# Two attentions moved from three-part bf16 rows to F32R row strips, with three single banks for first-pass scores and a ring of four for second scores

## The reference

```
Q = (query @ Wq.T).reshape(B, QL, HEADS, HEAD_DIM)
scores = einsum('bqhd,khd->bhqk', Q, K) * SCALE
attn = softmax(scores, axis=-1)
out = einsum('bhqk,khd->bqhd', attn, V)
```

## Time and profile before

| | |
|---|---|
| median of 3 runs | 2120.23 us (2119.72 to 2126.68) |
| profiled execution | 2117.09 us, its span 2115.3 us |
| granted TensorE clock, mean | 0.925 |
| busy: PE, DVE, ACT, POOL | 85%, 66%, 54%, 14% |
| a0: first matmul, first second-pass matmul, last work | 88.57, 112.17, about 885 us |
| a1: block starts, first second-pass matmul, last work | 1035.3, 1054.2, about 1287 us |

### The profile page before, as it was taken

How to read it: one execution, slowest core, us unless ns; L and a number is a source line. 1 busy time by engine, 2 the same in 40 slices (tenths; PEclk the granted TensorE clock), 3 DMA queues, 4 the chain that set the end, 5 groups by cost and what they waited for, 6 DMA issues and landing times. The chain is left out here.

```text
span 2115.3 us, 31356 instructions
## 1 busy us (share of the span) xinstructions
PE 1808.1 (85%) x9772; PEld 970.4 (46%) x9772; DVE 1399.7 (66%) x1846; ACT 1147.7 (54%) x2253; POOL 285.7 (14%) x447
## 2 busy tenths in 40 slices
PE   4499999999999999645699973499999999949997
PEld 3122222222222233133222221388888888748886
DVE  6487777877777888246467753666666666656665
ACT  3067767776777777513377762255445454424432
POOL 3210000000000000102111111211111111002223
PEclk8599999999999999856799986799999999979999
DMA  7201111111111200112312222100000000023432
GB/s 284 96 34 35 40 46 35 41 39 36 35 39 35 89 16 16 36 56 55 112 65 70 72 101 73 39 14 20 7 20 20 20 12 10 1 51 115 121 105 65
DMA packets 56274, 115.00 MB, mean 54 GB/s; under 512 B 7249, under 2 KB 21585, under 8 KB 54123
## 3 DMA queue, kind: packets, MB, share of 16 engines
q1 hardware_dynamic: 53715, 109.21, 15.9%
q10 hardware_dynamic: 2456, 4.46, 0.8%
HBM read 83.52 MB, written 30.12 MB: 54 GB/s over the span
## 5 line engine op out<-in xcount | busy, mean ns | idle before, releaser
L348 DVE TENSOR_REDUCE a_max_part<-psum 128x1 f32<-128x1024 f32 x640 | 759.6, 1220 | 253.8 <-PE psum L265 253.8
L389 ACT ACTIVATE a_probs<-psum 128x512 f32<-128x512 f32 x1280 | 675.1, 603 | 247.9 <-PE psum L309 242.7
L265 PE MATMUL psum<-a_k_rows,a_q_rows 96*128 96x512 bf16 x1280 | 399.6, 395 | 52.0 <-DMA a_q_rows<-q_parts 26.1
L309 PE MATMUL psum<-a_q_rows,a_k_rows 99*128 99x512 bf16 x1280 | 410.3, 386 | 29.6 <-ACT a_probs L389 29.3
L300 PE MATMUL psum<-a_probs,a_v_ext 128*32 128x512 f32 x2560 | 342.5, 607 | 6.1 <-ACT a_o_out L373 3.8
L265 PEld LDWEIGHTS psum<-a_k_rows,a_q_rows 96*128 96x128 bf16 x1280 | 98.8, 98 | 407.0 <-issue 193.0
L309 PEld LDWEIGHTS psum<-a_q_rows,a_k_rows 99*128 99x128 bf16 x1280 | 124.1, 98 | 268.8 <-ACT a_probs L389 155.4
L1548 PE MATMUL psum<-high_t_parts,high_gu 128*128 128x512 f32 x600 | 145.6, 393 | 6.8 <-DVE high_t_parts L1642 6.8
L1253 PE MATMUL psum<-wide_k_t,wide_q_t 128*128 128x512 f32 (+3 forms) x576 | 130.3, 353 | 1.7 <-DVE wide_id_bf L1452 1.7
L1548 PEld LDWEIGHTS psum<-high_t_parts,high_gu 128*128 128x128 f32 x600 | 113.6, 190 | 31.3 <-issue 7.3
L226 POOL TENSOR_TENSOR a_max_bf<-a_neg_max,a_zeros 128x4 bf16<-128x4 f32 x64 | 13.2, 206 | 849.0 <-DVE a_neg_max L352 849.0
(11 more groups left out here) (173 smaller groups left out, 1871.1 us busy)
## 6 DMA issues: line engine op xcount, KB each, us to landing
o<-a_o_out SPq DMA_DIRECT2D x64, 256.0 KB, 2.1
gu_in<-in_w_gu SPq DMA_DIRECT2D x25, 256.0 KB, 3.0
k_parts<-keys_parts SPq DMA_DIRECT2D x12, 512.0 KB, 6.5
a_k_rows<-k_parts SPq DMA_DIRECT2D x16, 384.0 KB
high_cw<-cw SPq DMA_DIRECT2D x24, 256.0 KB, 3.9
setup_k_in<-in_k SPq DMA_DIRECT2D x4, 1024.0 KB, 15.2
a_k_rows<-k_parts SPq DMA_DIRECT2D x16, 256.0 KB
a_v_in<-in_v SPq DMA_DIRECT2D x16, 256.0 KB, 14.8
```

The source lines that it names most:

```text
L265: mm = pe.matmul(psum[:, 2 * (n % 2) + j, :], q_rows[0:KROWS, b, q0:q0 + P], k_rows[0:KROWS, b, k0:k0 + 512], start=True, stop=True)
L309: pe.matmul(psum[:, bank_of(filling(j)), :], k_rows[0:SROWS, b, j * P:(j + 1) * P], q_rows[0:SROWS, b, half * QH:(half + 1) * QH], start=T ...
L348: dve.tensor_reduce(max_part[:, u % 2, c // nch, c % nch:c % nch + 1], psum[:, 2 * (n % 2):2 * (n % 2) + 2, :], AX.XY, ALU.max).then_inc(s ...
L389: act.activation(probs[:, j % pring, :], psum[:, bank_of(filling(j)), :], ACT.Exp).then_inc(exp_done, 1)
```

## The change

Keys and queries are no longer cut into bf16 parts. Each is cut in two F32R parts, high and low. A strip of 64 partitions holds three products of 16 rows each (48 rows, 51 with the maxima): high times high, high times low and low times high. The first half of a head's keys lies in the strip at partition 0, the second half in the strip at partition 64, and consecutive matmuls alternate between strips.

- GpSimd makes the key parts of each head (`split_keys`: three operations over `nkt * 64` columns), head by head, from a single buffer `k_in` that SP fills with four transfers (`load_k`); `setup` has no key split any more. `copy_v` works from a single buffer `v_in` too.
- The first pass uses three single banks (0 to 2) and reductions over 512 columns. The second pass has a ring of four banks (3 to 6).
- ScalarE copies the maxima into `max_row`, and SP moves them beside the queries by two transfers (`send_maxima`).
- VectorE, not ScalarE, copies out the sums (`take_sums`).
- TensorE's order inside a group is `slot`. All loops are written out. Resident heads: 3 in a0, 6 in a1. SP loads the sums of 15 heads before the last two units.
- In a0 the queries stay in SBUF and are spread by six transfers a head; in a1 they pass through DRAM, two transfers a head.

```diff
+        self.per_strip = nkt * P // 2
+        self.steps = nkt
+        self.shift = 12
+        self.turn_at = nkt - 6
+        self.ring = 4
+        self.first_ring = 3
+        self.early = 2
...
+    def load_k(self, sp, h):
+        keys = self.k_dram[HD * h:HD * h + HD, :]
+        for n in range(2):
+            part = keys[:, n * self.per_strip:(n + 1) * self.per_strip]
+            at = STRIP * n
+            sp.dma_start(self.k_in[at:at + 2 * HD, :],
+                         part.unsqueeze(0).broadcast_to([2, HD, self.per_strip])).then_inc(self.k_loaded, 16)
+            sp.dma_start(self.k_in[at + LOW_K:at + MROW, :], part).then_inc(self.k_loaded, 16)
...
+    def split_keys(self, pool, h):
+        b = h % self.nb
+        pool.wait_ge(self.k_loaded, 64 * (h + 1))
+        pool.tensor_tensor(self.k_rows[:, b, :], self.k_in[:, :], self.zeros[:, 0:1].broadcast_to([P, self.per_strip]),
+                           ALU.add).then_inc(self.k_high, 1)
+        pool.wait_ge(self.k_high, h + 1)
+        for s in range(2):
+            low = slice(STRIP * s + LOW_K, STRIP * s + MROW)
+            pool.tensor_tensor(self.k_rows[low, b, :], self.k_in[low, :], self.k_rows[low, b, :],
+                               ALU.subtract).then_inc(self.k_split, 1)
...
+        def heads_split(u):
+            return min(H, self.early + u + 1, nb + u // 2)
...
+            sent = self.early + 1
+            send_maxima(0)
+            for u in range(us):
+                h, half = u // 2, u % 2
+                if u + 1 < us:
+                    send_maxima(u + 1)
+                sp.wait_ge(self.o_full, u + 1)
+                sp.dma_start(self.o_dram[h, :, half * QH:(half + 1) * QH], self.o_out[:, half, :]).then_inc(self.o_stored[half], 16)
+                if half == 1 and h + nb < H:
+                    load_q(sp, q_rows[:, h % nb, :], h + nb, self.q_loaded[h % nb])
+                while sent < min(H, heads_split(u) + 1):
+                    sp.wait_ge(self.k_split, 2 * sent)
+                    self.load_k(sp, sent)
+                    sp.wait_ge(self.v_ready, sent)
+                    self.load_v(sp, sent)
+                    sent += 1
+                if u == us - 3:
+                    for n in range(2):
+                        sp.wait_ge(self.o_stored[n], 16 * (H - 1))
+                    load_sums(sp, o4, self.o_dram, 0, H - 1, self.o4_loaded)
...
+            for u in range(us):
+                if u + 1 < us:
+                    split_max(u + 1)
+                for h in range(done, heads_split(u)):
+                    self.copy_v(pool, h)
+                    self.split_keys(pool, h)
+                done = heads_split(u)
...
+            def first_chunk(n):
+                u, c = n // steps, n % steps
+                if n >= self.first_ring:
+                    pe.wait_ge(self.s1_free, n - self.first_ring + 1)
...
+                second_wait(u, j)
+                second_wait(u, j + 1)
+                second_chunk(u, j)
+                second_chunk(u, j + 1)
+                if one < self.chunks:
+                    first_chunk(one)
+                    first_chunk(one + 1)
+                if j + 2 == self.turn_at and u + 1 < us:
+                    turn_maxima(u + 1)
+                second_wait(u, j + 2)
+                second_chunk(u, j + 2)
+                if one < self.chunks:
+                    first_chunk(one + 2)
+                second_wait(u, j + 3)
+                second_chunk(u, j + 3)
+                if one < self.chunks:
+                    first_chunk(one + 3)
+                if g > 0:
+                    pv_group(u, g - 1)
+                elif u > 0:
+                    pv_group(u - 1, groups - 1)
...
+            for u in range(us):
+                for s in range(steps):
+                    if s == 4 and u > 0:
+                        take_sums(u - 1)
+                    n = u * steps + s + ahead
+                    if n < self.chunks:
+                        first_pass_chunk(n)
```

More of the change, by code:

```diff
@@ new lines, in _ @@
+            pool.wait_ge(self.v_const, 2)
+            self.copy_v(pool, 0)
+            for h in range(1, self.early):
+                self.split_keys(pool, h)
+                self.copy_v(pool, h)
+            done = self.early
+            split_max(0)
+            for u in range(us):
+                if u + 1 < us:
+                    split_max(u + 1)
+                for h in range(done, heads_split(u)):
+                    self.copy_v(pool, h)
+                    self.split_keys(pool, h)
+                done = heads_split(u)
@@ L330, in _ @@
[L330 to L341 removed]
+                mm.then_inc(self.pv_done, 1)
@@ new lines, in slot @@
+            def slot(u, g):
+                j = group * g
+                one = u * steps + 4 * g + ahead
+                second_wait(u, j)
[19 more added lines that the diff above has]
+                    pv_group(u - 1, groups - 1)
@@ new lines, in _ @@
+            put_row(0)
+            for u in range(us):
+                for j in range(nkt):
+                    p = u * nkt + j
+                    if j == self.turn_at and u + 1 < us:
+                        put_row(u + 1)
+                    act.wait_ge(self.s2_full, p + 1)
+                    if p >= self.pring and p % group == 0:
+                        act.wait_ge(self.pv_done, (p - self.pring) // group + 1)
+                    act.activation(self.probs[:, p % self.pring, :], psum[:, self.bank_of(u, self.filling(j)), :],
+                                   ACT.Exp).then_inc(self.exp_done, 1)
@@ new lines, in project, with _ @@
+        if q_out is not None:
+            @block.sync
+            def _(sp):
+                heads = P // HD
+                for c in range(DC):
+                    sp.wait_ge(high_done, 2 * c + 2)
+                    sp.wait_ge(low_done, 2 * c + 2)
+                    for at, src in ((0, q_high), (HD, q_low), (2 * HD, q_high)):
+                        sp.dma_start(q_out[heads * c:heads * (c + 1), at:at + HD, :], src[:, c, :].bitcast(F32)).then_inc(stored, 16)
+                for c in range(DC):
+                    sp.wait_ge(k_taken, 2 * c + 2)
+                    sp.dma_start(k_out[c * P:(c + 1) * P, :], k_sb[:, c, :]).then_inc(stored, 16)
@@ L1700, in adaln_two_layers, with load_q @@
-            project(nc, psum, "p0", h_t, wq, 1, [q0_parts], None, keys_stored, 16 * 3 * 4)
-        with ExitStack() as part:
-            o4 = part.enter_context(nc.sbuf_tensor("o4_0", [P, DC, 4, T], F32))
-            attention_core(nc, psum, ident_bf, "a0", nk0 // P, 4, k0_parts, q0_parts, i["v0"], o0, o4)
-            merge_heads(nc, psum, "m0", 4, o4, o0, den0, i["wo0"], gates[:, 0, :], x)
+            o4 = part.enter_context(nc.sbuf_tensor("o4_0", [P, DC, 4, T], F32))
+            with ExitStack() as core:
+                attention = Attention(nc, core, psum, ident_bf, "a0", nk0 // P, 3, i["k0"], i["v0"], o0)
+                q_high = core.enter_context(nc.sbuf_tensor("q_high", [P, DC, T], F32R))
+                q_low = core.enter_context(nc.sbuf_tensor("q_low", [P, DC, T], F32R))
+                def load_q(sp, rows, h, loaded):
+                    at = HD * (h % 8)
+                    for n in range(2):
+                        for m, src in enumerate((q_high, q_low, q_high)):
+                            row = STRIP * n + HD * m
+                            sp.dma_start(rows[row:row + HD, :].bitcast(F32), src[at:at + HD, h // 8, :].bitcast(F32)).then_inc(loaded, 16)
+                with ExitStack() as front:
+                    setup(nc, psum, i["c"], i["wmod"], i["ident"], ident, ident_bf, mod_col, mod_row, gates, i["x"], x,
+                          i["ln_w"], ln_w[:, :], attention)
+                    wq = front.enter_context(nc.sbuf_tensor("wq", [P, DC, 1, D], F32))
+                    normalise(nc, psum, "n0", x, ident, False, mod_col[:, 2:4], mod_col[:, 0:2], h_t,
+                              loads=[(wq[:, :, 0, :], chunks(i["wq0"]))])
+                    project(nc, psum, "p0", h_t, wq, 1, q_high, q_low)
+                with nc.Block() as block:
+                    attention.run(block, load_q, 6, o4)
```

591 lines of the change are left out of this document (229 added, 362 removed).

## The result

The changed kernel takes 2273.62 us (median of 4 runs, 2270.23 to 2276.41). Beside it on the same chip the kernel before took 2120.32 (2119.72 to 2126.68). The ratio is 1.0715, 95% interval 1.0689 to 1.0741. It is 153 us slower; the forecast was 108 us slower, 2228, with a range up to 2285.

What follows compares the result with a forecast made beforehand. TensorE, busy 99% in a0's steady part, was read as the bound before the change. The terms 11 - 10 - 14.5 + 15 + 113 - 6 = +108.5 gave 2228 us against the median, range 2130 to 2285.

Steps and rivals of the forecast that it cites:

- Part 1: a0's groups: one chain of first-pass matmuls, reduction and values, 3.0 us a group against 2.90; +11 us (-18 to +40).
- the wait behind the sums: Before a0's last unit: its maxima stand behind the sums of 15 heads in SP's queue; +15 us (0 to +18).
- The jumps' 10 us: a0's loop: the two jumps back, 5.2 us each, go; -10 us.
- Part 2: Start of a0: block 10 us earlier, second pass begins 39 us after it, at 97.5; -14.5 us (-20 to -8).
- load until about 15, 13.6: Start of a0: head 1 loaded until about 15 us after the block, then GpSimd's key split takes 13.6 us.
- maxima through SP, 4.5: Start of a0: moving the first maxima through SP takes 4.5 us before the second pass begins.
- Part 4: a1: maxima wait behind sums and loads in SP's queue, early units also for GpSimd; 364 against 251 us, +113 (+60 to +145).
- A: a1 and before the last units: maxima never late, a1's units 6.3 us, 2081 us in all; chance 0.13.
- B: a0: VectorE sets the pace, 21.6 us a unit, -73 in place of +11, 2144 us in all; chance 0.13.
- F3's wait: a0's group: the fourth first-pass matmul waits until VectorE has reduced the group's first, since there are three banks.
- C: a0: changing between strips costs TensorE 0.2 us a group extra, unit 26, +50 more, 2278 us; chance 0.12.
- Part 5: The rest: merge_heads loads one head's sums, not four, and project has fewer parts; -6 us (-12 to 0).

Runs made afterwards that it cites:

- the kernel after all the mending: All the order edits together, with GpSimd's key split in a1 in two steps, against the changed kernel: 2050.0 us, ratio to the kernel before 0.9645 to 0.9692.

## Why the prediction was right, and where its sizes were off

The direction and the mechanism held: a0's gain is small, a1 pays for order in SP's queue. The forecast was 45 us short, and a1 alone is 45 short. That the other errors nearly cancel is luck: the start was 20 us worse than forecast, the rest of a0 27 us better, and the stages between and behind 11 us worse.

**Part 1, a0's group.** The chain is as described. Forecast 2.88 to 3.11 and 3.0 taken, measured 2.94 to 2.99; its parts 0.78 (0.72 if strips load and run at once, 0.90 if not), 0.74 (0.75) and 0.43 (0.41). I leaned to serial weight loads (3.06); the strips overlap, as the run with the strips one at a time shows by 0.2 us a group. Times 31 units, the 0.8 us that a unit came out shorter is most of the 27 us by which this stretch was better than forecast (-11 against +16); the wait behind the sums was 8.9, not 15. The jumps' 10 us fit.

**Part 2, the start.** The step that failed is "load until about 15, 13.6" and "maxima through SP, 4.5". The block began 4.2 us later than I put it (62.7). The keys of head 1 were there 26 us after it and not 15, since SP issues all of a0's queries first and the load itself takes 12 (issued at 74.91 to 77.3, split from 89.0). So GpSimd was done 41.4 us after the block and not 31, which passed the 34 at which the first pass ends: +7.4. From the turning to TensorE it took 13.2 us and not 4.5, behind the next head's keys: +8.7. 4.2 + 7.4 + 8.7 = 20.3, against the 19.6 by which the start was worse. The run that sends these maxima ahead of the keys shows the last part: 2.7 us from issue to TensorE.

**Part 4, a1.** The terms against the stores of sums in the trace:

| | forecast | measured |
|---|---|---|
| block to the first sums | 38 | 43.0 |
| units 1 to 8 | 109 | 122.8 |
| units 9 to 20 | 113 | 136.7 |
| units 21 to 29 | 63 | 66.4 |
| unit 30, with the sums | 37 | 35.0 |
| sums of unit 30 to the merge | 4 | 6.4 |

The plain unit is 7.09 (7.1), the wait at the sums 28 us (30). What was mis-sized is the half clock, which I had left out and put into the high end at 15 us. In the units with keys or queries from unit 7 on, the stretch from TensorE's start to the sums takes 4.83 us in 12 of 14 and 4.1 to 4.3 in two, instead of 3.35. In units 1 to 6 the stretch from the turning to the sums takes 3.67 instead of 2.68. Together that is about 25 of the 46 us. Another 5 were lost up to the first sums; the rest is spread over issues and landings, such as 3.22 us from the maxima's issue to TensorE in the unit above against 2.65, and is not taken apart further. In these units TensorE waits for the maxima for 0.6 to 5.6 us, mostly 2 to 4, and in units 1 to 6 another 3.9 for `split_max`; the clock is 0.56 in the early units and 0.61 in the pairs. The earlier trace rows had shown it: 3.3 us without work, then a group 1.5 us longer. The rows were read, the number was right, and I did not ask how often it would happen.

**Rivals.** A (maxima never late) is the kernel after all the mending: SP's transfers are in order, and only with the order changed do units of 6.3 appear. B (VectorE sets a0's pace) fails on F3's wait, and nearly holds once F3 stands behind the values: 22.2 a unit where 21.6 was forecast, with VectorE 92% busy and still waiting 0.22 us in most groups. C (changing between strips costs extra) is refuted: it gains 2.2 us a unit, by the one run with the strips one at a time.

**Part 5** was -6 and came out at +5: the merge after a0 gained 3.6, but a1's values are now waited for at the end of `project`, and a1's block began only 2.3 us earlier.

## What to carry to other kernels

Count a wait of TensorE together with the clock behind it, and multiply by how often it occurs: here a wait of about 3 us cost up to 4.5. Where small transfers feed the next step, write down everything ahead of them in their queue and on the engine that makes them; another queue, and the same work cut into pieces that fit between two of them, made up most of the 224 us here (41 are a0's order of matmuls), while what is transferred stayed the same. And check an order loop by loop: F3 behind the values gave 1.4 us a unit in a0 and cost 2.9 in a plain unit of a1, half of it clock.

## What the runs showed of the hardware

- TensorE at 100% busy, with F32R matmuls of 48 and 51 rows all in the strip at partition 0 (and value matmuls of 128 rows between them), stayed at half clock for 1400 us. Matmuls of the same shapes given out over both strips, mostly one at a time, ran at the full clock (1.00 from 200 to 800 us). Why is open.
- At a0's start, with both strips in use and TensorE 100% busy, the clock rose about 13 us after the second pass began in the changed kernel, and 31 and 32 us after it in two other runs.
- Two F32R row strips overlap: 4.59 against 5.58 us a group at half clock, 2.95 against 3.17 at the full clock (the second in one run).
- Two small transfers on ScalarE's queue passed the sums that stood in SP's (5.8 us from issue to use, against 11.4 behind them, and 2.65 behind one store of sums in a1). That they passed is read from the first issue of the sums, 18.6 us before TensorE had the maxima, where it is 24.2 in one queue. They cost ScalarE 1.4 us of issue.
- A head's keys and values (1 MB, the key part in rows of 16 and 32 partitions) took 12 us to land in a0, and anything behind them as long.
